# A macaron block on one core: pass two's first group ahead of the last maxima, one head spread and the second mixture's weight loads moved to earlier stages

## What is computed

```python
x = x + 0.5 * mixture(layernorm(x))
x = x + attention_layer(layernorm(x))
x = x + 0.5 * mixture(layernorm(x))      # the same weights as the first

# attention_layer: 16 heads of 8 channels, a key is at most 128 tokens back
h = x + attention(layernorm(x, ln1)) @ wo
out = h + (silu(n @ w1) * (n @ w3)) @ w2        # n = layernorm(h, ln2)

# mixture: top 2 of 8 experts per token; experts 0-3 are MLPs, 4-7 are KAN layers
probs = softmax(x @ gate_W); rw, sel = top_k(probs, 2); rw = rw / rw.sum(-1)
mlp(x) = gelu(x @ W1 + b1) @ W2 + b2
kan(x) = hills(ln(hills(ln(x)) @ W0 + b0)) @ W1 + b1     # 8 hills 1 - tanh^2 per channel
```

## Time and profile before

| | us |
|---|---|
| median of 3 runs (665.77, 665.86, 671.14) | 665.86 |
| the profiled execution | 667.89 |
| its span, first to last instruction | 666.1 |
| PE busy | 572.4 (86%) |
| DVE busy | 469.9 (71%) |
| ACT busy | 389.5 (58%) |
| POOL busy | 265.2 (40%) |

### The profile page before, as it was taken

The page is one execution under the profiler, slowest core; times in us unless marked ns, Lnnn a source line. Parts: engine busy times, 40 slices in busy tenths (PEclk is TensorE's granted clock), DMA queues, the critical chain, the costliest instruction groups (busy, mean ns, idle before and its releaser), DMA issues. The chain is left out here.

```text
span 666.1 us, 19481 instructions
## 1 busy us (share of the span) xinstructions
PE 572.4 (86%) x6576; PEld 507.4 (76%) x6577; DVE 469.9 (71%) x1192; ACT 389.5 (58%) x924; POOL 265.2 (40%) x305
## 2 busy tenths in 40 slices
PE   6787999999999478888789888988689999999980
PEld 5776889999988455766678674687588899999970
DVE  6743777778877477699477778558348787778864
ACT  2325888889864158700457433214268888889853
POOL 6035456656644255820000002120354566656540
PEclk8768999999999669899899999996799999999996
DMA  8982122000100030000000000039910011000106
GB/s 246 341 318 75 61 77 78 24 28 28 32 17 16 23 117 3 3 3 15 14 4 4 4 2 1 1 116 330 347 41 18 28 32 32 24 28 28 32 17 193
DMA packets 41240, 46.58 MB, mean 70 GB/s; under 512 B 7216, under 2 KB 33184, under 8 KB 40160
## 3 DMA queue, kind: packets, MB, share of 16 engines
q1 hardware_dynamic: 32224, 34.00, 16.0%
q0 software_dynamic: 4736, 9.71, 5.5%
q10 hardware_dynamic: 4224, 2.10, 1.1%
HBM read 35.69 MB, written 10.09 MB: 69 GB/s over the span
## 5 line engine op out<-in xcount | busy, mean ns | idle before, releaser
L865 PE MATMUL k_y_ps<-kan_w,k_basis 128*128 x1056 | 126.9, 280 | 8.3 <-DVE k_basis L962 5.4
L865 PEld LDWEIGHTS k_y_ps<-kan_w,k_basis 128*128 128x128 f32 x1056 | 123.4, 195 | 10.2 <-issue 10.0
L855 PE MATMUL k_z_ps<-kan_w,k_basis 128*128 x528 | 119.9, 380 | 1.1 <-issue 1.1
L1128 ACT ACTIVATE k_sig<-k_h1T 128x256 f32<-128x256 f32 x264 | 84.4, 402 | 53.1 <-DVE k_h1T L987 52.9
L855 PEld LDWEIGHTS k_z_ps<-kan_w,k_basis 128*128 128x128 f32 x528 | 97.7, 190 | 13.8 <-issue 1.6
L962 DVE SCALAR_TENSOR_TENSOR k_basis<-k_sig 128x512 f32<-128x512 f32 x132 | 85.8, 691 | 15.7 <-ACT k_sig L1128 15.7
L1121 ACT ACTIVATE k_sig<-k_h0T 128x128 f32<-128x128 f32 x280 | 59.2, 293 | 8.7 <-DVE k_h0T L950 8.6
L1797 ACT ACTIVATE got<-p_ps 128x960 f32<-128x960 f32 (+1 forms) x44 | 39.3, 944 | 26.5 <-PE p_ps L1655 26.5
L681 POOL DMA_INDIRECT y_rows<-k_y,k_rows x33 | 33.2, 1005 | 48.1 <-DVE k_y L994 30.1
L1726 DVE TENSOR_REDUCE p_minus_max<-p_ps 128x6 f32<-128x960 f32 (+1 forms) x44 | 45.9, 1116 | 6.0 <-PE p_ps L1620 5.0
L833 PE MATMUL m_z_ps<-m_xT,m_w 128*128 128x128 f32 x304 | 43.2, 288 | 5.9 <-ACT m_w L1150 4.2
(11 more groups left out here) (270 smaller groups left out, 1112.3 us busy)
## 6 DMA issues: line engine op xcount, KB each, us to landing
kan_w<-in_L_ffn_kan_sl_W_dram SPq DMA_DIRECT2D x16, 1024.0 KB, 10.6
x_rows<-got SPq DMA_DIRECT2D x4, 1024.0 KB, 12.8
mlp_w<-in_L_ffn_mlp_W_dram SPq DMA_DIRECT2D x2, 1024.0 KB, 5.9
mlp_w<-in_L_ffn_mlp_W_dram SPq DMA_DIRECT2D x8, 256.0 KB, 6.6
got<-y_rows SPq DMA_DIRECT2D x8, 256.0 KB, 4.9
got<-y_rows ACTq DMA_DIRECT2D x8, 256.0 KB, 5.5
xs<-in_L_attn_x_dram SPq DMA_DIRECT2D x4, 256.0 KB, 3.4
s_cos<-in_cos_dram SPq DMA_DIRECT2D x8, 128.0 KB
```

Of the source, the lines that this page charges most:

```text
L855: last = nc.tensor.matmul(z_ps, basis0[:, g], k.kan_w0[:, bass.ds(e, 1), g], start=(g == 0), stop=(g == G - 1))
L865: last = nc.tensor.matmul(y_ps, basis1[:, g, c], k.kan_w1[:, bass.ds(e, 1), c, g], start=(g == 0 and c == 0), stop=(g == G - 1 and c == F2 ...
L1128: ins = nc.scalar.activation(sig1[:, g], h1T[:], ACT.Sigmoid, bias=float(-GRID[g]))
```

## The change

Three edits. First, `spread_q(3)` leaves `project` and becomes the first thing on ACT's list in `attend`; the semaphore `q_spread` becomes one of the attention's, and `row_scores` waits for it where a group reaches into chunk 3. Second, on PE the six unused products ahead of the last maxima go, and `key_scores(0)` stands ahead of `turn_maxima(1)`; the wait for ACT's second copy moves to group 1, ahead of `by_key_sums(0)`, since `by_values(1)` is the first to write the bank of the turned maxima. On ACT the second half's copy and cast come behind the first group's exponentials, and its last cast behind the second group's. Third, `load_mlps` and the four `load_kan` of the second mixture move from SP's list in `route` to one in `finish_attention`; `moe_weights` for n = 1 is called ahead of that block, so `moe` and `attention` are written as one function.

```diff
@@ route, SP @@
-                load_mlps(sp, k, a, n)
                 if n == 0:
+                    load_mlps(sp, k, a, n)
                     load_shared(sp, k, a)
-                load_kan(sp, k, a, n, 0)
+                    load_kan(sp, k, a, n, 0)
...
                 sp.wait_ge(xn_ready, NT)
                 sp.dma_start(rows[0], xn).then_inc(k.rows_in_dram[n], 16)
-                load_kan(sp, k, a, n, 1)
+                if n == 0:
+                    load_kan(sp, k, a, n, 1)
                 sp.wait_ge(xh_ready, NT)
                 sp.dma_start(rows[1], xh).then_inc(k.rows_in_dram[n], 16)
-                load_kan(sp, k, a, n, 2)
-                load_kan(sp, k, a, n, 3)
+                if n == 0:
+                    load_kan(sp, k, a, n, 2)
+                    load_kan(sp, k, a, n, 3)
@@ project, ACT @@
                 take_v(3)
-                spread_q(3)
@@ attend, PE @@
                     blocks, n = GROUPS[t], len(GROUPS[t])
+                    if blocks[-1] >= LAST_CHUNK * BCH:
+                        pe.wait_ge(s.q_spread, HG * (LAST_CHUNK + 1))
...
                     row_scores(t)
+                pe.wait_ge(k_spread, HG * NT // PART)
                 pe.wait_ge(reduced, 2 * (N - 1))
-                keep_running(nc, k, ps[:, scores_set(N - 2), 0:P], 6)
+                key_scores(0)
                 turn_maxima(1)
-                pe.wait_ge(m_copied, 2)
-                pe.wait_ge(k_spread, HG * NT // PART)
-                key_scores(0)
                 for t in range(N):
                     if t + 1 < N:
                         key_scores(t + 1)
+                    if t == 1:
+                        pe.wait_ge(m_copied, 2)
                     if t:
                         by_key_sums(t - 1)
                     by_values(t)
@@ attend, ACT @@
+                spread_heads(nc, s.q_bd, s.qT, s.sel, LAST_CHUNK, s.q_spread)
                 for g in range(NT // PART):
                     spread_heads(nc, s.k_bd, s.kT, s.sel, g, k_spread)
...
+                first_part(0)
+                second_part(0)
+                act.preload_act_table(ACT.Exp)
+                exponentials(0)
+                first_part(1)
+                exponentials(1)
+                second_part(1)
+                for t in range(2, N):
+                    exponentials(t)
@@ finish_attention @@
+            @block.sync
+            def _(sp):
+                load_mlps(sp, k, a, 1)
+                for e in range(E2):
+                    load_kan(sp, k, a, 1, e)
@@ attention_and_mixture @@
             attend(nc, k, a, s)
+        moe_weights(nc, k, ctx, 1)
         finish_attention(nc, k, a, s)
+        route(nc, k, a, 1, None)
+        moe_blocks(nc, k, a, 1, None, out)
```

More of the change, by code:

```diff
@@ L2119, in macaron @@
             s = attention_weights(nc, k, weights)
[L2120 to L2122 removed]
+            with ExitStack() as first:
+                moe_weights(nc, k, first, 0)
+                route(nc, k, a, 0, s)
+                moe_blocks(nc, k, a, 0, s, None)
+            attention_and_mixture(nc, k, a, s, out)
 _INS = ["L0_attn_x", "L0_attn_wq", "L0_attn_wk", "L0_attn_wv", "L0_attn_wo", "L0_attn_w1", "L0_attn_w2",
```

20 lines of the change are left out of this document (7 added, 13 removed).

## The result

Sixteen runs of each kernel, on one chip: the changed kernel's median is 660.74 us (657.12 to 665.74), the kernel before 669.54 (665.70 to 673.45). The ratio is **0.9871, 95% interval 0.9849 to 0.9894**: 1.3% less time. The forecast, as a ratio, was 657.9 / 665.86 = 0.9880. The profiled execution took 659.14 us (span 657.3, mean granted clock 0.944), where before it was 667.89 (span 666.1, clock 0.924): 8.8 us off the span.

A forecast was written before the change was run, and what follows sets the result against it. Three places bound it: ACT's last query spread ending `project`, alternating PE/ACT waits between the passes, and slow gathers behind weight loads at the second mixture's start. 0.6 + 4.2 + 3.2 = 8.0 us, so 665.86 - 8.0 = 657.9; 8-in-10 range 656.0 to 660.9.

The forecast's parts named there:

- Part one: End of `project`: without the last query spread, PE instead of ACT sets the block border; 0.6 us less, bounds 0 and 1.0.
- Part two: Pass two's first group: key scores and `exp` no longer wait for maxima, copy, casts and table load; 4.2 us less.
- the growth from 3.2 to 4.5: Pass two: `exp` starts 3.16 us earlier, the third group's exponentials 4.5; from the vanished 2.06 us wait and half-clock products.
- The last maxima's later way: Their way by ACT, POOL and DRAM gets later, hidden because they are first read at the tenth group, 24 us on.
- Part three: Second mixture's start: weights loaded earlier, so gathers go out sooner and land faster; first W1 product 3.2 us earlier.
- PE-bound loops carry the shift to the end: Second mixture behind the first KAN tile: order and waits stay as before, so the 3.2 us gain is kept.
- The sum: Whole kernel: 0.6 + 4.2 + 3.2 = 8.0 us less, bounds 5.6 and 9.6.
- 2.0 lower by other causes: The base: the runs' median, 665.86 us, against the profiled execution's 667.89; the 8.0 us were subtracted from it.
- The gather that stays slow: Rival at the second mixture's start: gather takes 5.7 us despite an empty queue, leaving 0.7 of part three; 660.4, chance 0.14.
- The smaller gain in pass two because the clock falls anyway: Rival: only the earlier start is gained, 3.2 us for part two; 660.3 with part three at its bound, chance 0.13.
- Instruction pages behind the weights: Rival in `finish_attention`: two pages stall engines behind the loads, up to 682.7 us; chance 0.06 together with another full-queue effect.
- the rule in the Trainium skill: Engines fetch instructions in 16 KiB blocks over a DMA queue; a branch to a page not held stalls the engine.

The follow-up runs named there:

- u_before: The kernel before with the four block counts loaded as 16-bit values and nothing else changed; median 667.41 us beside 667.10 for the kernel before.
- c_after: The changed kernel with the loaded block counts asserted to be at least 1; median 661.75 us beside 666.85 for the kernel before, ratio 0.9921.
- u9_tail: The changed kernel with 16-bit count loads, plus 8 unused products ahead of each mixture's last KAN group; median 657.17 us beside 667.10 for the kernel before.
- u9b_tail: The kernel of u9_tail run again; median 655.86 us against 659.65 for u_after2 beside it.
- u5_pe_order: The changed kernel with 16-bit count loads, but ScalarE keeps its old order at the border; median 663.57 us beside 667.10 for the kernel before.
- u6b_no_start: The changed kernel with 16-bit count loads, without the 8 unused products at the second mixture's start; no median given, column d 209.80 us against 209.93.
- e3_loads: Part three alone put into the kernel before, with the block counts asserted; median 668.19 us against 668.08 for the kernel before with the assertions.
- u_after2: The changed kernel with the block counts loaded as 16-bit values, run once more as a base; median 659.65 us beside 665.87 for the kernel before.
- 16-bit kernels: The kernels labelled with u, before or changed, that load the block counts as 16-bit values; their base u_before has median 667.41 us beside 667.10.
- u4_spread_border: Parts one and two without part three, put into the kernel before, with 16-bit count loads; median 661.41 us beside 665.87 for the kernel before.

## Where the prediction was right, and the steps that failed

**Part one (0.6 us): right.** 0.59 in each profile, hidden spread and all.

**Part two (4.2, bounds 3.2 to 4.7): right in its size, its reason half right.** Columns b and c of the compared pair give 2.06 + 2.52 = 4.58. Over all the profiles b + c is 17.0 to 18.3 us in five of the six without part two, 15.5 in the sixth (u_before, where the clock doesn't fall), and 12.46 with part two, or 13.96 to 13.99 in the three of eleven in which the clock fell behind the border (c_after, u9_tail, u9b_tail). At full clock on both sides part two is worth 15.53 - 12.46 = 3.07 us; the rest is that the old 2 us wait brings the low clock in five of six profiles. The forecast put the growth from 3.2 to 4.5 down to two things, the 2.06 us wait that disappears and the half clock behind it. u_before has the wait and no low clock, and its exponentials stand so on the timeline (its last maximum ends at 297.18 + 23.06 = 320.24):

```profile
323.40 1.83 ACT L1797 ACTIVATE got<-p_ps 128x960 f32<-128x960 f32 x2
325.84 1.83 ACT L1797 ACTIVATE got<-p_ps 128x960 f32<-128x960 f32 x2 [0.60 <-PE p_ps L1655]
328.27 1.83 ACT L1797 ACTIVATE got<-p_ps 128x960 f32<-128x960 f32 x2 [0.60 <-PE p_ps L1655]
```

The first is 3.16 us behind the last maximum and the third 8.03, against 0.10 and 4.97 in the changed kernel: 3.06 us at both. The wait alone adds nothing to the gain; the growth is the clock's. The last maxima's later way cost nobody anything, as forecast.

**Part three (3.2, bounds 2.4 to 3.9): right up to the first W1 product, wrong behind it.** The gathers land as forecast: 2.4 to 2.8 us behind the start of their issue in every kernel with part three whose profile shows the landing, 5.4 to 6.3 in the kernels without. The start is then bound by the unused products, and in the compared pair the first W1 product comes 3.5 us earlier (43.65 against 47.19 us behind the attention's last product group). Column d is 2.70 us less. The step that failed is "PE-bound loops carry the shift to the end": 0.8 of the 3.5 us are lost again, all of it ahead of the second KAN group. There the chain that ended last does not go over TensorE. In the changed kernel it has

```profile
474.20 1.27 issue
475.47 0.04 POOLq L697
475.51 0.17 issue
475.68 2.98 DMA y_rows<-m_y,m_rows
...
479.88 1.51 another core or an unknown queue
```

with ScalarE's weight copies between and behind them; before, the store to `y_rows` held the chain for 2.30 us at that place and TensorE had most of the rest. The first KAN group shows it over the runs: in seven of the eleven kernels with part three the first W1 product starts anywhere from 43.65 to 46.01 us behind the attention's last product group, and the first KAN group between 59.25 and 60.16 without following it (u5_pe_order 45.22 and 59.25, u6b_no_start 43.89 and 59.94). Only where the product starts later than 46.2 does the group come later too (60.6 to 62.0, in c_after, e3_loads and u_after2). How large part three is stays open within a microsecond: in column d the 16-bit kernels give 2.3 us between the quickest of each kind and 3.5 between the means, the medians of u4_spread_border and u_after2 1.8.

**The sum (8.0): right.** The three terms measure 0.59 + 4.58 + 2.70 = 7.87 in the pair. The other 0.93 of the 8.80 stand at places that the change doesn't touch, and the forecast left them out: 0.57 ahead of the end of `project`, 0.69 at pass one's start, 1.27 in the rest of pass two, less 1.60 in the last group and the tail. The 0.69 and the 1.60 go with a stretch at 1.2 GHz that one profile has and the other has not. The 1.27 don't: both profiles have one such stretch there, with a granted clock of 0.88 from 372 to 386 us before and from 366 to 380 now. Most of it is two pauses of TensorE in the middle of a product group, which move the key scores behind them by 0.85 and 0.58 us; the first stands so on the timeline of before:

```profile
342.53 0.34 PE L1672 MATMUL p_ps<-got,s_v_bd 128*32 128x160 f32 x3 [0.53 <-issue]
```

No engine ends the pause, and its cause stays open. Over the eighteen profiles such differences come and go without regard to the parts: the rest of pass two takes 58.1 to 61.1 us, column e 21.2 to 23.7. So that 8.0 and 8.8 lie as close as they do is in part luck.

**The time in microseconds (657.9 against 660.74): 2.8 us too low, and the step that failed is the base.** The forecast subtracted its sum from "the median of the runs, which is 2.0 lower by other causes", 665.86, and gave no cause. It was the median of three runs, of which two happened to be quick. With sixteen runs the same kernel's median is 669.54, 3.7 us higher, and the gain was 0.8 us larger than the sum. The other groups gave 666.85, 668.90, 667.10 and 665.87 for the same kernel, with single runs from 660.7 to 674.1. 660.74 lies above the sum's own bounds (656.3 to 660.3) and 0.2 us inside the edge of the 8-in-10 range (656.0 to 660.9), which is luck. The subtraction held, what it was subtracted from did not: against the profiled execution the forecast was 659.9, and the changed kernel's took 659.14; as a ratio it was 0.9880, inside the interval. That interval, 1.1 to 1.5% less time, is also above the 1% that the forecast gave 0.64.

**The rivals.** The gather that stays slow: out, 2.4 to 2.8 us from issue to landing. The smaller gain in pass two because the clock falls anyway: it happens, in three of eleven profiles, with b + c 1.5 us longer; against the profile before that leaves 3.1 us, just under the lower bound of 3.2. Whether the six unused products that part two takes out would have kept the clock up in these three, no run shows. Instruction pages behind the weights: out. Two pages and a smaller packet were fetched, TensorE had no idle time there that it lacked before, and the stage took 38.35 to 38.38 us in all eighteen profiles, with the loads and without. The loads took 28 us (388 to 416) and not some 36 (394 to 430), which changes nothing else.

Of the rule in the Trainium skill (Runtime: NRT & Kernel Launch, Instruction fetch mechanics) only the fetches are seen in this stage; no run shows a stall there.

## What to carry over

Where short waits stand one behind another on alternating engines, take out of the list everything that the first work behind them doesn't read; a microsecond of TensorE's idle time can cost about as much again in the low clock behind it (u5_pe_order: 3.1 us of wait, 5.9 us lost), so price a wait with the clock's stretch, and call that part likely, not sure. Bulk loads belong where neither a small dependent transfer nor a gather is behind them in the queue. Follow a shift past its first product: an earlier start is kept only while the chain behind it stays on the same engine. And measure a change of one per cent by the same distances in the traces of many runs, against a base of many runs: the median of three lay at the lowest of the five later medians of the same kernel and 3.7 us under the highest.

## What the runs showed of the hardware

- Asserting four loaded counts (8 sequencer instructions) delayed TensorE by 1.15 us (4.50 to 5.65); loading them as 16-bit values with a stride, without any assertion, still by some 0.6 (5.18 to 5.23), since the load takes 1.00 us and not 0.34.
- 10.75 MB of weights beside the attention's last stage moved at 315 to 415 GB/s in the stage table, with a DMA share near 1.0, and lengthened no instruction group there; in the routing before, the loads and the row writes together ran at 308 to 400 GB/s from 450 to 480 us.
- A gather of 128 rows issued by GpSimd into empty queues landed 2.4 to 2.8 us behind the start of its issue, and the next one, issued 0.3 us behind its end, as fast; behind the weight loads it was 5.4 to 6.3.
- Eight unused products in a 2.5 us gap kept TensorE at 2.4 GHz through six of six last groups (3.83 us each); without them the group took 5.33 us or more in all fifteen profiles in the first mixture and in ten of fifteen in the second.
